# Graph network kernel: node numbers as places in the row table, strided copies made from DRAM, 109 rows of edges

## What is computed

```python
h = maximum(layernorm(x), 0)
h = batchnorm(h, g0, b0)
for W1, b1, gamma, beta, W2, b2 in layers:      # two layers
    agg = segment_sum(h[src], dst, N)           # sum over the edges of a target
    h = relu(batchnorm((h + agg) @ W1 + b1, gamma, beta))
    h = relu(h @ W2 + b2)
out = x + relu(h)
```

## Time and profile before

| | |
|---|---|
| median of 3 runs | 2775.24 us (2773.72 to 2776.81) |
| profiled execution | 2784.43 us, its span from first to last instruction 2782.6 us |
| mean granted clock of TensorE | 0.940 of full speed |
| gathers by POOL | 224 raw, 1648 in the walks |
| DMA | 734.28 MB, 579.47 MB read from HBM and 152.59 MB written |

### The profile page before, as it was taken

One profiled execution on the slowest core, in us unless ns is written; L12 is line 12 of the kernel. 1 busy time (PEld: TensorE's weight loads), 2 busy tenths in 40 slices (PEclk: granted clock), 3 DMA queues, 4 the chain that ended last, 5 costly groups with the idle time before them and its releaser, 6 DMA issues.

```text
span 2782.6 us, 30723 instructions
## 1 busy us (share of the span) xinstructions
PE 2371.1 (85%) x10215; PEld 1827.6 (66%) x10215; DVE 1739.1 (62%) x3502; ACT 551.3 (20%) x1605; POOL 1815.2 (65%) x1894
## 2 busy tenths in 40 slices
PE   1466777999999999999979566699999999988979
PEld 1134433878877777777758444588888888776767
DVE  7999997755555555555548577555555555544459
ACT  8975544300000000000009311000000000000038
POOL 2058777777777777777740477677777777777720
PEclk8687766999999999999989899999999999999999
DMA  9387998888888888888848999888888888888868
GB/s 309 141 261 224 285 306 254 250 260 251 253 253 255 254 255 254 254 254 254 254 153 279 328 334 325 285 283 286 287 284 284 287 285 282 260 254 253 253 203 270
DMA packets 309364, 734.28 MB, mean 264 GB/s; under 512 B 41510, under 2 KB 183730, under 8 KB 309198
## 3 DMA queue, kind: packets, MB, share of 16 engines
q0 software_dynamic: 149184, 550.97, 63.2%
q1 hardware_dynamic: 160014, 181.25, 20.8%
HBM read 579.47 MB, written 152.59 MB: 263 GB/s over the span
## 4 chain that ended last, share of the span: by engine, by line
PE 51%; DMA 23%; POOL 8%; SPq 8%; ACT 5%; issue 4%; DVE 1%; DVEq 0%; ACTq 0%; POOLq 0%
PE agg_ps L830 35%; DMA rows<-node_rows,src_all 17%; SPq L617 7%; PE sort_ps L955 6%; PE sort_ps L872 5%; POOL rows L697 5%; DMA rows<-node_rows,raw_list 4%; PE sort_ps L876 2%; DMA raw_more<-node_rows,raw_list 2%; PE agg_ps L779 2%; ACT acc L1001 2%; POOL raw_more L679 2%; ACT lane_code L988 1%; ACT lane_code L977 1%; POOL rows L679 1%
## 5 line engine op out<-in xcount | busy, mean ns | idle before, releaser
L697 POOL DMA_INDIRECT rows<-node_rows,src_all x1648 | 1558.2, 946 | 642.6 <-issue 346.4
L830 PE MATMUL agg_ps<-rows,work 128*128 128x256 f32 (+1 forms) x7004 | 1630.3, 387 | 188.9 <-DMA rows<-node_rows,src_all 140.8
L830 PEld LDWEIGHTS agg_ps<-rows,work 128*128 128x128 f32 x7004 | 1297.7, 191 | 494.3 <-issue 133.9
L1582 DVE SCALAR_TENSOR_TENSOR acc<-agg_ps,in_first,acc 128x256 f32 (+1 forms) x286 | 138.7, 485 | 944.1 <-PE agg_ps L830 856.7
L1032 ACT ACTIVATE bn_root<-bn_var 128x2 f32<-128x2 f32 x3 | 0.6, 203 | 1860.2 <-DVE bn_var L1168 1860.2
L679 POOL DMA_INDIRECT rows<-node_rows,raw_list x124 | 129.2, 1042 | 174.8 <-DMA node_rows<-acc 137.3
L1534 DVE TENSOR_TENSOR work<-lane_code,lane_ps 128x1024 f32<-128x1024 f32 (+1 forms) x206 | 228.1, 1107 | 1.0 <-issue 1.0
L955 PE MATMUL sort_ps<-early,work 128*128 128x256 f32 x784 | 175.3, 388 | 22.1 <-ACT work L1117 11.5
L955 PEld LDWEIGHTS sort_ps<-early,work 128*128 128x128 f32 x784 | 140.2, 194 | 57.5 <-issue 25.6
L1543 DVE TENSOR_TENSOR work<-lane_code,lane_ps 128x640 f32<-128x640 f32 x206 | 167.7, 814 | 0.0
L1117 ACT ACTIVATE work<-acc,bn_shift,bn_scale 128x128 f32<-128x128 f32 x392 | 166.5, 485 | 3.3 <-DVE bn_shift L1179 2.8
(11 more groups left out here) (246 smaller groups left out, 1844.8 us busy)
## 6 DMA issues: line engine op xcount, KB each, us to landing
node_rows<-acc SPq DMA_DIRECT2D x113, 260.0 KB, 6.3
rows<-node_rows,src_all POOLq DMA_INDIRECT x1648, 4.4
node_rows<-acc SPq DMA_DIRECT2D x27, 910.0 KB, 4.3
node_rows<-acc SPq DMA_DIRECT2D x57, 390.0 KB, 5.4
node_rows<-acc SPq DMA_DIRECT2D x28, 650.0 KB, 8.6
node_rows<-acc SPq DMA_DIRECT2D x114, 130.0 KB, 4.6
acc<-in_x SPq DMA_DIRECT2D x13, 896.0 KB, 11.0
rows<-in_x SPq DMA_DIRECT2D x13, 896.0 KB, 7.3
```

What stands on the lines that cost most here:

```text
L697: pool.indirect_dma_start(tile_rows(k, 0, ROWS_OF[t] * DP), None, tables[layer][0:NPOS if t >= LAST_STRIDED else TABLE, :], bass.IndirectO ...
L830: mm = pe.matmul(bank[:, 0:width], hot[:, unit * P:(unit + 1) * P], tile_rows(k, row, width), start=(start and n == 0), stop=(stop and n = ...
L1582: dve.scalar_tensor_tensor(to, sums, lanes[:, g:g + 1], to, ALU.mult, ALU.add).then_inc(sums_added, 1)
```

## The change

- A node's place is its number: `NPOS` is 12600 instead of 13440, without gaps between partitions. `places` stores a block as 128 neighbouring rows, so that a store from SBUF has pieces of one row (1040 bytes).
- A strided copy is read from the natural table in DRAM and written to DRAM, as 16 pieces of n rows (n from 16 to 38), 19 DMAs for a group. SP waits for the group's rows to be stored before it issues one. Beside the dense part the copies of group i begin behind the store of chunk 2 i + 2.
- `table_stored` becomes one semaphore per group (`rows_stored`); POOL waits for all, SP and ACT for the group's.
- `add_self` waits for the group's rows alone, not for copies.
- `LR` is 1950 instead of 1932, so there are 109 rows of edges; 14 stay raw, and `TWICE`, `BESIDE` and `COPIES_UNTIL` are as before.
- The places need no arithmetic in DVE's setup: three operations go, one copy with a cast comes, and POOL's `part_place` goes.
- The zeros of unused places are fewer and smaller.

```diff
-PITCH = NB + 7
-NPOS = P * PITCH
+NPOS = 12600
...
-LR = 1932
+LR = 1950
...
-PAD_SRC = 1000 * P + P - 1
-SRC_CAP = 14000
+PAD_SRC = 14000
+SRC_CAP = 13500
...
         def places(table, b0, b1):
-            return table[0:NPOS, :].rearrange("(p b) f -> p b f", b=PITCH)[:, b0:b1, :]
+            return table[b0 * P:b1 * P, :].rearrange("(b p) f -> p b f", p=P)
...
-        def strided_places(table, stride, b0, b1, of):
-
-            lanes = stride // math.gcd(stride, PITCH)
-            for lane in range(lanes):
-                for first in range(b0, min(b0 + stride, b1)):
-                    n = len(range(first, b1, stride))
-                    yield (places_of(table, place_in(stride, lane * PITCH + first),
-                                     [(lanes * PITCH // stride, P // lanes), (1, n)]),
-                           of(first, n, stride)[lane:P:lanes])
-
-        def copies_of_blocks(table, b0, b1):
+        def copied_to(stride, i):
+
+            return (i * GROUP * P if i < GROUPS else NPOS) // (16 * stride) * (16 * stride)
+
+        def copies_of_group(table, i):
+
             for stride in STRIDES:
-                yield from strided_places(table, stride, b0, b1, lambda first, n, step: block_rows(first, first + (n - 1) * step + 1, step))
+                first, end = copied_to(stride, i), copied_to(stride, i + 1)
+                n = (end - first) // (16 * stride)
+                for place in range(first, first + stride):
+                    yield (places_of(table, place_in(stride, place), [(n, 16), (1, n)]),
+                           places_of(table, place, [(n * stride, 16), (stride, n)]), 16 * n)
...
-            copies = [(to, of) for i in range(GROUPS) for to, of in copies_of_blocks(tables[0], i * GROUP, (i + 1) * GROUP)]
-            for n, (to, of) in enumerate(copies):
+            copies = [(i, to, of) for i in range(GROUPS) for to, of, _ in copies_of_group(tables[0], i)]
+            sp.wait_ge(spare_stored, 2 * SPARE)
+            for n, (i, to, of) in enumerate(copies):
+                sp.wait_ge(rows_stored[i], ROWS_STORED[0][i])
                 beside_tile = n * COPIES_UNTIL // len(copies)
...
+            def copy_next():
+                nonlocal issued
+                i, to, of, n = copies[issued]
+                sp.wait_ge(rows_stored[i], ROWS_STORED[1][i])
+                sp.dma_start(to, of).then_inc(group_stored[i], 16)
+                issued += 1
+                return n
+
             for c in range(NCH - 1):
                 store_rows(1, c, y_out, (c + 1) * CH)
                 rows_beside = 0
-                while c % 2 + c // 2 and rows_beside < BESIDE:
-                    i, to, of = next(copies)
-                    sp.dma_start(to, of).then_inc(group_stored[i], 16)
-                    rows_beside += of.shape[0] * of.shape[1]
+                while rows_beside < BESIDE and 2 * copies[issued][0] + 1 < c:
+                    rows_beside += copy_next()
             store_last_rows()
-            for i, to, of in copies:
-                sp.dma_start(to, of).then_inc(group_stored[i], 16)
+            while issued < len(copies):
+                copy_next()
...
         def add_self(layer):
                 width = D + 1 if layer == 0 else D
                 act.wait_ge(self_ready, 1)
-                act.wait_ge(table_stored, TABLE_DMAS[layer])
-                if layer == 0:
-                    act.wait_ge(copies_stored, COPIES)
                 for b in range(NB):
-                    if layer and b % GROUP == 0:
-                        act.wait_ge(group_stored[b // GROUP], GROUP_COPIES)
+                    if b % GROUP == 0:
+                        act.wait_ge(rows_stored[b // GROUP], ROWS_STORED[layer][b // GROUP])
...
-            setup(dve.tensor_scalar(key_ints[:, 0:GIVEN], src_int, P - 1, None, ALU.bitwise_and))
-            setup(dve.tensor_scalar(src_places, src_int, 7, None, ALU.logical_shift_right))
+            setup(dve.tensor_scalar(key_ints[:, 0:LR], dst_int[:, 0:LR], P - 1, None, ALU.bitwise_and))
+            setup(dve.tensor_copy(src_rows, src_int))
             setup(dve.tensor_tensor(self_edges, src_int[:, 0:LR], dst_int[:, 0:LR], ALU.is_equal))
-            dve.wait_ge(setup_done, done)
-            setup(dve.scalar_tensor_tensor(src_rows, key_ints[:, 0:GIVEN], float(PITCH), src_places, ALU.mult, ALU.add))
-            dve.wait_ge(setup_done, done)
-            setup(dve.tensor_scalar(key_ints[:, 0:LR], dst_int[:, 0:LR], P - 1, None, ALU.bitwise_and))
```

More of the change, by code:

```diff
@@ L215 @@
 assert PAIRS_BESIDE * RAW_GROUPS >= NPAIR and RAW % RAW_GROUP == 0 and 0 < LAST_EDGES <= P and 4 * SORT + RAW_INSIDE * DP <= RING * DP
-assert SRC_CAP > NPOS + UP and all(NPOS % s == 0 and i + 1 == min(s, 6) - 2 for i, s in enumerate(STRIDES))
+assert PAD_SRC + UP >= SRC_CAP > NPOS + UP and NPOS > NPAD and all(NPOS % s == 0 and i + 1 == min(s, 6) - 2 for i, s in enumerate(STRIDES))
 assert NB * (QUARTER + 1) <= RING * DP and 4 * SORT <= RING * DP and X_SLOTS * CH * D <= RING * DP
@@ L284, in build @@
         part_col = sb("part_col", [P, 1])
-        part_place = sb("part_place", [P, 1])
         ident = sb("ident", [P, P])
@@ L388, in build @@
         group_stored = [sem(f"group_stored{i}") for i in range(GROUPS)]
-        table_stored = sem("table_stored")
+        rows_stored = [sem(f"rows_stored{i}") for i in range(GROUPS)]
         copies_stored = sem("copies_stored")
@@ L518, in build @@
         SPARE = 16 * sum(1 for _ in spare_places(tables[0]))
-        GROUP_COPIES = 16 * sum(1 for _ in copies_of_blocks(tables[0], 0, GROUP))
+        GROUP_COPIES = 16 * sum(STRIDES)
         COPIES = GROUPS * GROUP_COPIES
-        TABLE_DMAS = [16 * NCH, 16 * (2 * NCH - 1 + len(LAST_PIECES))]
+        ROWS_STORED = [[32] * GROUPS, [64] * (GROUPS - 1) + [16 * (3 + len(LAST_PIECES))]]
         BN = 4
-        POOL_SETUP = 5
-        SETUP_PLACES = 7
-        SETUP_LANES = 20
+        POOL_SETUP = 4
+        SETUP_PLACES = 5
+        SETUP_LANES = 18
         SRC_LIST = [(tr_ps[0], 0, 4), (tr_ps[1], 4, T)]
@@ L564, in store_rows @@
                 b0, b1 = c * CH, (c + 1) * CH
-                sp.dma_start(places(tables[t], b0, b1), block_rows(b0, b1)).then_inc(table_stored, 16)
-            def copies_by_group():
-                for i in range(GROUPS):
-                    for to, of in copies_of_blocks(tables[1], i * GROUP, (i + 1) * GROUP):
-                        yield i, to, of
+                sp.dma_start(places(tables[t], b0, b1), block_rows(b0, b1)).then_inc(rows_stored[c // 2], 16)
             def store_last_rows():
@@ L575, in store_last_rows @@
                     sp.wait_ge(y_out, b1)
-                    sp.dma_start(places(tables[1], b0, b1), block_rows(b0, b1)).then_inc(table_stored, 16)
+                    sp.dma_start(places(tables[1], b0, b1), block_rows(b0, b1)).then_inc(rows_stored[GROUPS - 1], 16)
             def store_last(dram, sbuf, stored, first):
@@ L605, in _ @@
                 sp.dma_start(bias_b[i], bb.partition_broadcast(P)).then_inc(weights_loaded, 16)
-            copies = copies_by_group()
+            copies = [(i, to, of, n) for i in range(GROUPS) for to, of, n in copies_of_group(tables[1], i)]
+            issued = 0
+            def copy_next():
[5 more added lines that the diff above has]
+                return n
             for c in range(NCH - 1):
@@ L672, in _ @@
             pool.wait_ge(spare_stored, 2 * SPARE)
-            pool.wait_ge(table_stored, TABLE_DMAS[0])
+            for i in range(GROUPS):
+                pool.wait_ge(rows_stored[i], ROWS_STORED[0][i])
             for g in range(RAWS):
@@ L702, in _ @@
             for layer in range(2):
-                pool.wait_ge(table_stored, TABLE_DMAS[layer])
+                for i in range(GROUPS):
+                    pool.wait_ge(rows_stored[i], ROWS_STORED[layer][i])
                 if layer:
```

18 lines of the change are left out of this document (10 added, 8 removed).

## The result

The changed kernel takes 2799.5 us (median of 4 runs, 2794.4 to 2801.1) where the kernel before takes 2774.5 in the same comparison: 1.0083 times as long, 95% interval 1.0069 to 1.0097. It is **slower by 25 us**; 9.9 faster was forecast.

A forecast was written before the change was run, and what follows sets the result against it. POOL's chain of gathers, 1.25 us each, was taken to bound the kernel, with three joints. -20.0 + 0.6 + 5.4 + 4.1 = -9.9 us, from a median of 2775.2 to 2765; range 2743 to 2840.

The forecast's parts named there:

- the price of a copied row with its source in DRAM: Strided copies, now DRAM to DRAM: a row costs what it did from SBUF, 0 us; within 5%, chance 0.50.
- rival (a): POOL's wait for table 1's copies becomes long: rows up to 1.3 times dearer, 2797 at 1.2 times; chance 0.18.
- Mixed traffic shows no lower rate: Argument against dearer copies when gathers and copies read DRAM while the copies write it; no size of its own.
- the wait at the strided gathers: Sign at POOL's wait for table 1's copies: about 20 us instead of 11.7 if right, 40 and more if wrong.
- Two rows of gathers less: Walks of both layers: one row of 8 gathers fewer in each, at 1.25 us a gather, -20.0 us.
- First raw gather: Start of layer 0's raw part: the last store, in one-row pieces, takes 2.9 us instead of 2.3, +0.6 us.
- Small stores: Table 1's stores in one-row pieces, 9 of 14 chunks counting: +5.4 us on the end of the copies.
- Own sums: ACT's scaling of node rows no longer waits for copies: 0, covered by POOL; otherwise worth 4.6 us.
- DVE's setup: Fewer setup operations start the sort 3.5 to 5.2 us earlier; hidden by POOL, 0.
- The raw part's room of some 36 us: Raw part of layer 0: 266 GB/s on average where 301 were reached, so dearer copies have some 36 us of room.
- further apart than 1.25: Sign of a wrong copy price: raw gathers more than 1.25 us apart.
- The later start of the copies: Table 1's first two copies wait for stored rows and move into the full DMA stretch: +4.1 us on the copies' end.

The follow-up runs named there:

- The kernel with SBUF sources: Changed kernel with the copies of groups 0 to 5 in 128 pieces, read from SBUF at one row a packet: 2782.9 us, ratio 1.0017 to the kernel before.
- the profiled one with small stores: Kernel before, each chunk of the natural table stored as two DMAs in one-row pieces of 1040 bytes: 2785.1 us, ratio 1.0029; its profiled execution took 2780.4 us.
- the run with `BESIDE` alone: Changed kernel with at most four blocks' worth of copied rows between two stores of table 1 instead of eight: 2811.3 us, ratio 1.0120 to the kernel before.

## Why the prediction was wrong

**The step that failed** is the price of a copied row with its source in DRAM, put at the old price, 0 us. With the same packets, a source in DRAM costs 24 us for six groups of seven, 28 for all: 28/160 = 18%, where gain and loss met at 6%. By the profiled joints it is somewhat more: from the last gather of layer 0 to the first strided one 375.4 us with the source in DRAM, 347.1 from SBUF, 28 for six groups, 33 for seven. The reason given was that loads and stores cost the same per byte, so that the engine and not the memory behind it makes a packet's time. That only says what a packet costs with DRAM on one side; no row of before had one with DRAM on both, and the equality could not speak for it. The 18% are in the prediction's own unit, 16 us for each 10%; the engine time of the packets in the raw part grew by 6%. This is rival (a), at about 1.2 times, for which 2797 was worked out; 2799.5 was measured. That the two lie so close is in part luck, as some of the 25 us is not accounted for below. "Mixed traffic shows no lower rate", held against it, was a reading of traffic with the same shortcoming. Of the signs, the wait at the strided gathers came out between both, 30.7 us (20 for right, 40 and more for a wrong price); the other 15 us stand at the first natural gather, which no sign named.

By the rate of the Trainium skill, "DMA: Bandwidth & Descriptors", section "Latency and other measured facts", a copied row would by the prediction's estimate have cost 1.53 times the old one. The copies here ran at 230 GB/s when they were almost alone, 7 to 11% above its 207 to 214. What was too high was the price made of it: it sets a rate of copies alone against the 328 of a mixture with gathers and stores. By the same division 230 would give 1.43, and the price beside gathers, by the times, was 1.18.

**The rest of the sum.** Two rows of gathers less: -9.7 and -8.9 in the walks, where -10 each was put. First raw gather: +0.9 for +0.6. Small stores: 8 for 6.0, but by its profile at the first natural gather and not at the end of the copies. Own sums: 0, right, as is DVE's setup (the raw part ends as far from its beginning as before). The raw part's room of some 36 us held as well: it took the dearer copies without a wait. Two readings were off, and no term hangs on them: raw gathers were 1.375 us apart before the change already (224 in 308.0 us), so that to find them further apart than 1.25 could be no sign; and behind 1476 stand the stores of 12 of the 14 chunks of table 1, not of half of it.

**What remains.** -9.9 + 28 leaves 18, or 23 with the 33 of the profiles, of 25. The kernel with SBUF sources, which still takes one group from DRAM (4 us of the 28), should have been 6 us faster than before, and is 5 slower. The later start of the copies, put at 4.1, does not explain these 11. At its last stores, 114.9 us after the last gather of layer 0 (118.3 before), this kernel had issued 32 of its 133 copies, 12288 rows, and the kernel before 61 of 217, 14080 rows: 1792 rows are 1.9 MB, 5.7 us at 328 GB/s, with 3.4 us less to do it in.

Profile against profile nothing is missing. From the last gather of layer 0 to the first strided one this kernel takes 347.1 us and the kernel before 339.5, 7.6 more, where 5.4 + 4.1 + 4 had been worked out; the changed kernel takes 373.8, 34.4 more, where 9.5 + 28 (or 33) had been. So the two ways of counting differ by about the 9.2 us by which the profiled execution of before, with its wait of 11.7 us for copies, stood above its median. A usual execution of before has perhaps no such wait, as the profiled one with small stores has none. This is argued: no other execution of before was profiled, and how the 11 us divide was not measured.

The stores that stand behind copies in SP's queue were not in the sum at all; it was said only that a store waits for DVE longer than for the landing before it. They do delay the first natural gather by 15 us, but, as the run with `BESIDE` alone shows, this costs nothing while the copies end later still.

## What to carry to other kernels

That loads and stores cost alike does not make it free to move the source of a copy from SBUF to DRAM: price it by a run with DRAM on both sides, or take the dearer case as likely, above all where the margin is 6%. A gain that is spread over the kernel and a cost that falls on one stretch with full DMA engines are not to be summed before asking how much of the cover in that stretch is left; here a kernel that had 5 to 8 us to pay for its copies came to pay 50. After such a change the sizes that cover the copies (how many gathers come first, how much is let in between stores) have to be set anew, in both kernels, before the change itself is judged.

## What was not expected of the hardware

- With several rows in a packet instead of one of 1040 bytes, the whole time fell by 36 us from DRAM and 31 from SBUF, with the packets of the queue down from 173238 to 102582 and 117430. The Trainium skill, "DMA: Bandwidth & Descriptors", section "Why small descriptors are slow (HBM only)", holds joining consecutive descriptors into a packet worth it only up to 256 bytes each. What was changed here is not quite that, as the pieces themselves became longer; for copies beside gathers, longer pieces paid far above 256 bytes.
- The price of copies from DRAM to DRAM depended on how far apart the pieces of one DMA lie: beside raw gathers 264 GB/s at a share of 1.08 with pieces all over the table, 291 at 1.03 with pieces in a seventh of it, a wait of 20.9 us and 22 us of the time. Why, no run here tells.
- A lower rate can stand beside an equal or higher DMA share: 305 GB/s at 1.05 against 328 at 1.04, 264 at 1.08 against 291 at 1.03. Where only the memory differs, the share falls a little with the rate (313 at 1.02, 331 at 1.06). The share alone didn't tell here how much the engines moved.
